# Time mixing of an eight-stage network on one core: one product per batch on GpSimd, two denominators on GpSimd, residual on TensorE or VectorE

## The reference, cut to what matters

```
xn = ln(x);  xx = shift(xn)                       # previous position
k = mix(xn, xx, mu_k) @ Wk;  v = ... @ Wv;  r = sigmoid(... @ Wr)
scan over positions, per batch and channel, carry (aa, bb, pp):
    qq  = max(pp, u + k);   e1 = exp(pp - qq);   e2 = exp(u + k - qq)
    wkv = (e1*aa + e2*v) / (e1*bb + e2)
    qq2 = max(pp + w, k);   e1b = exp(pp + w - qq2);   e2b = exp(k - qq2)
    aa, bb, pp = e1b*aa + e2b*v,  e1b*bb + e2b,  qq2
x = x + (r * wkv) @ Wo
ei = ln(x)                                        # feeds the expert layer
```

## Time and profile before

| | |
|---|---|
| median of 3 runs | 1217.03 us (1211.10 to 1218.83) |
| the profiled execution | 1211.25 us, of which 1208.9 us from the first to the last instruction |
| mean granted TensorE clock | 0.981 |
| PE busy | 1102.3 us (91%) |
| DVE busy | 931.1 us (77%) |
| ACT busy | 812.0 us (67%) |
| POOL busy | 234.9 us (19%) |

### The profile page before, as it was taken

One profiled execution on the slowest core, in us unless ns is written; L12 is line 12 of the kernel. 1 busy time (PEld: TensorE's weight loads), 2 busy tenths in 40 slices (PEclk: granted clock), 3 DMA queues, 4 the chain that ended last, 5 costly groups with the idle time before them and its releaser, 6 DMA issues.

```text
span 1208.9 us, 20220 instructions
## 1 busy us (share of the span) xinstructions
PE 1102.3 (91%) x7428; PEld 614.3 (51%) x7436; DVE 931.1 (77%) x1521; ACT 812.0 (67%) x1292; POOL 234.9 (19%) x332
## 2 busy tenths in 40 slices
PE   7978899999999989989999899898888888898987
PEld 3333344444444445467765354466666666463354
DVE  5997798777777677767775578699999896576966
ACT  6885655555555654755576646888888776868774
POOL 1000000000000001200000013487878776000000
PEclk9999999999999999989999999899999998999999
DMA  6000112121221000000000000000000000000002
GB/s 177 1 0 1 56 56 67 65 62 61 62 61 61 27 1 0 10 1 2 2 1 1 1 0 9 1 3 2 2 3 2 16 2 2 9 1 1 1 1 69
DMA packets 26361, 27.17 MB, mean 22 GB/s; under 512 B 4171, under 2 KB 17308, under 8 KB 26268
## 3 DMA queue, kind: packets, MB, share of 16 engines
q1 hardware_dynamic: 25936, 25.91, 7.3%
q10 hardware_dynamic: 332, 0.01, 0.0%
HBM read 23.30 MB, written 2.62 MB: 21 GB/s over the span
## 4 chain that ended last, share of the span: by engine, by line
PE 61%; DVE 19%; ACT 12%; issue 6%; POOL 1%; DMA 0%; ACTq 0%; DVEq 0%
PE psum L723 9%; PE psum L734 9%; PE psum L726 4%; PE psum L87 4%; PE psum L983 4%; PE psum L955 3%; PE psum L1634 2%; PE psum L1965 2%; DVE arena L2151 2%; PE psum L1382 2%; DVE N L2160 2%; ACT ln_std L114 2%; ACT ln_std L116 2%; PE psum L105 1%; ACT N L2065 1%
## 5 line engine op out<-in xcount | busy, mean ns | idle before, releaser
L762 ACT ACTIVATE arena<-psum 128x512 f32<-128x512 f32 x128 | 69.5, 594 | 114.5 <-PE psum L723 114.5
L723 PE MATMUL psum<-arena,weights 128*128 128x512 f32 x256 | 122.2, 600 | 1.7 <-DVE N L128 1.0
L734 PE MATMUL psum<-arena,weights 128*128 128x512 f32 x256 | 120.3, 592 | 0.0
L620 DVE SCALAR_TENSOR_TENSOR arena<-diff,vecs,N 128x512 f32<-128x512 f32 x128 | 95.1, 745 | 0.0
L682 DVE SCALAR_TENSOR_TENSOR arena<-arena,psum 128x512 f32<-128x512 f32 x64 | 43.9, 686 | 62.8 <-PE psum L734 62.8
L2065 ACT ACTIVATE N<-N 128x1024 f32<-128x1024 f32 x64 | 67.8, 1059 | 32.2 <-DVE N L2160 31.6
L1975 PE MATMUL psum<-ident,N 128*128 128x128 f32 x512 | 73.0, 288 | 13.3 <-POOL N L2120 12.7
L723 PEld LDWEIGHTS psum<-arena,weights 128*128 128x128 f32 x256 | 48.2, 191 | 62.4 <-issue 57.9
L734 PEld LDWEIGHTS psum<-arena,weights 128*128 128x128 f32 x256 | 48.6, 190 | 61.4 <-issue 61.4
L1965 PE MATMUL psum<-arena 32*128 32x128 f32 x1024 | 77.2, 290 | 1.6 <-ACT arena L2043 1.4
L2061 ACT ACTIVATE arena<-psum 128x1024 f32<-128x1024 f32 x64 | 65.6, 1024 | 19.2 <-PE psum L1975 19.0
(11 more groups left out here) (330 smaller groups left out, 2491.0 us busy)
## 6 DMA issues: line engine op xcount, KB each, us to landing
arena<-tw_rows SPq DMA_DIRECT2D x64, 256.0 KB, 3.1
out_dram<-arena SPq DMA_DIRECT2D x8, 256.0 KB, 3.6
arena<-in_L_attn_a_x_dram SPq DMA_DIRECT2D x3, 512.0 KB, 6.7
weights<-in_L_attn_a_eWk_dram SPq DMA_DIRECT2D x1, 1024.0 KB, 6.0
arena<-in_L_attn_a_x_dram SPq DMA_DIRECT2D x2, 256.0 KB, 3.9
weights<-in_L_attn_a_eWr_dram SPq DMA_DIRECT2D x1, 512.0 KB, 9.9
tw_rows<-arena SPq DMA_DIRECT2D x2, 128.0 KB, 2.7
tw_rows<-arena SPq DMA_DIRECT2D x1, 256.0 KB, 3.5
```

The source lines that it names most:

```text
L620: op = nc.vector.scalar_tensor_tensor(mixed[:, n % 4, a, :], k.diff[:, q % 2, :], k.vec((f"cm_k{e}", f"cm_r{e}")[a]), before, ALU.mult, AL ...
L723: op = nc.tensor.matmul(k.bank[2 * (n % 2) + h][:], k.eWk[:, e, h * P:(h + 1) * P], mixed[:, n % 4, 0, :], start=True, stop=True)
L734: op = nc.tensor.matmul(k.bank[4 + n % 2][:], k.eWv[:, e, h, :], ks[:, (2 * (n % 2) + h) * CH:(2 * (n % 2) + h + 1) * CH], start=(h == 0), ...
L762: op = nc.scalar.activation(kr[:, h * CH:(h + 1) * CH], k.bank[2 * (n % 2) + h][:], ACT.Relu)
```

## The change

- VectorE no longer makes e2*V (L443). GpSimd makes it, for all four batches, once d(b) is done (so p is free), V(b) is taken and the last exponential of batch b is there. VectorE's numerator (L445) waits for it through a new semaphore, `wkv_part`.
- For batches 2 and 3 GpSimd also adds e2 to e1*bb in place, and `over` reads that sum from SBUF. den(2) and den(3) are gone from TensorE, and `totals[b]` is used for b = 0 and 1 only.
- On TensorE, den(0) still follows K3, then come V3, R0, den(1), R1, R2, R3. On ScalarE, the takes of V3 and R0 to R3 stand between the last weights, each one or more places earlier.
- The residual: for batches 0 and 1 TensorE first multiplies Y by the identity into `backs[b]` and adds Wo's product onto it, and ScalarE copies the sum to Y (`keep`); for batches 2 and 3 VectorE adds as before, counted by a new semaphore, `wkv_added`. On VectorE the four results now stand one behind another.
- The second norm's waits are renumbered accordingly.

```diff
--- before.py
+++ after.py
@@ -307,9 +307,7 @@
                 nc.tensor.matmul(k.bank[n % 4][:], k.wA[:, j, :], before, start=False, stop=True).then_inc(k.kvr, 1)
 
         def den(b):
-            total = totals[b % 2]
-            if b >= 2:
-                pe.wait_ge(k.wkv_ln, b - 1)
+            total = totals[b]
             pe.wait_ge(k.wkv_exp, 4 * b + 4)
             for c in range(2):
                 nc.tensor.matmul(total[:, c * CH:(c + 1) * CH], k.ident[:], e2[b % 2][:, c * CH:(c + 1) * CH], start=True, stop=False)
@@ -319,23 +317,25 @@
             op.then_inc(k.wkv_total, 1)
 
         def out(b):
-            pe.wait_ge(*((k.kvr_out, 2 * len(place)) if b < 2 else (k.wkv_ln, b + 1)))
+            pe.wait_ge(*((k.kvr_out, 2 * len(place)) if b < 2 else (k.wkv_ln, b - 1)))
+            if b < 2:
+                for c in range(2):
+                    nc.tensor.matmul(backs[b][:, c * CH:(c + 1) * CH], k.ident[:], k.Y[:, half[b][c]], start=True, stop=False)
             pe.wait_ge(k.wkv_out, b + 1)
             for c in range(2):
-                nc.tensor.matmul(backs[b][:, c * CH:(c + 1) * CH], k.wA[:, 3, :], R[:, half[b][c]], start=True, stop=True).then_inc(k.wkv_prod, 1)
+                nc.tensor.matmul(backs[b][:, c * CH:(c + 1) * CH], k.wA[:, 3, :], R[:, half[b][c]], start=(b >= 2), stop=True).then_inc(k.wkv_prod, 1)
 
         pe.wait_ge(k.mix_fold, 6)
         pe.wait_ge(k.pads_set, 2 * B)
         for kind, b in (("K", 0), ("K", 1), ("V", 0), ("V", 1), ("K", 2), ("V", 2), ("K", 3)):
             mix(kind, b)
         den(0)
+        mix("V", 3)
+        mix("R", 0)
         den(1)
-        mix("V", 3)
-        for b in range(B):
+        for b in range(1, B):
             mix("R", b)
-        den(2)
         out(0)
-        den(3)
         out(1)
         for c in range(2):
             after.center(pe, c)
@@ -372,10 +372,15 @@
             nc.scalar.activation(buf, buf, ACT.Exp, scale=-1.0).then_inc(k.wkv_exp, 1)
 
         def over(b):
-            act.wait_ge(k.wkv_total, b + 1)
-            nc.scalar.activation(K[:, at[b]], totals[b % 2], ACT.Ln, scale=2.0).then_inc(k.wkv_ln, 1)
+            act.wait_ge(*((k.wkv_total, b + 1) if b < 2 else (k.wkv_part, 2 * b)))
+            nc.scalar.activation(K[:, at[b]], totals[b] if b < 2 else e1b[b % 2], ACT.Ln, scale=2.0).then_inc(k.wkv_ln, 1)
             act.wait_ge(k.wkv_ln, b + 1)
             nc.scalar.activation(K[:, at[b]], K[:, at[b]], ACT.Exp, scale=-1.0).then_inc(k.wkv_rden, 1)
+
+        def keep(b):
+            for c in range(2):
+                act.wait_ge(k.wkv_prod, 2 * b + c + 1)
+                nc.scalar.activation(k.Y[:, half[b][c]], backs[b][:, c * CH:(c + 1) * CH], ACT.Copy).then_inc(k.wkv_y, 1)
 
         take("K", 0)
         take("K", 1)
@@ -391,28 +396,40 @@
             weight(1, n)
         take("V", 2)
         take("K", 3)
-        for n in range(4):
-            weight(2, n)
+        weight(2, 0)
+        weight(2, 1)
+        take("V", 3)
+        weight(2, 2)
+        weight(2, 3)
+        take("R", 0)
         weight(3, 0)
         weight(3, 1)
-        take("V", 3)
-        take("R", 0)
+        take("R", 1)
         weight(3, 2)
-        take("R", 1)
+        take("R", 2)
         weight(3, 3)
-        take("R", 2)
         take("R", 3)
         activations(act, k, "natural_log_exp_and_others")
-        over(0)
-        over(1)
-        over(2)
+        for b in range(B):
+            over(b)
+        keep(0)
         act.wait_ge(k.wkv_num, B - 1)
-        act.wait_ge(k.wkv_total, B - 1)
         for c in range(2):
             after.square(act, c)
-        over(3)
+        keep(1)
         for c in range(2, 4):
             after.square(act, c)
+
+    @block.gpsimd
+    def _(pool):
+        for b in range(B):
+            pool.wait_ge(k.wkv_d, b + 1)
+            pool.wait_ge(k.kvr_out, 2 * place[f"V{b}"] + 2)
+            pool.wait_ge(k.wkv_exp, 4 * b + 4)
+            nc.gpsimd.tensor_tensor(p[b % 2], e2[b % 2], V[:, at[b]], ALU.mult).then_inc(k.wkv_part, 1)
+            if b >= 2:
+                pool.wait_ge(k.wkv_e1bb, b + 1)
+                nc.gpsimd.tensor_tensor(e1b[b % 2], e1b[b % 2], e2[b % 2], ALU.add).then_inc(k.wkv_part, 1)
 
     @block.vector
     def _(dve):
@@ -433,15 +450,14 @@
             nc.vector.tensor_tensor_scan(bb[:, 1:L + 1], e1b[s], e2b[s], 0.0, ALU.mult, ALU.add).then_inc(k.wkv_step, 1)
             dve.wait_ge(k.kvr_out, 2 * place[f"V{b}"] + 2)
             nc.vector.tensor_tensor(aa[:, 1:L + 1], e2b[s], V[:, at[b]], ALU.mult).then_inc(k.wkv_step, 1)
-            dve.wait_ge(k.wkv_step, 5 * b + 2)
+            dve.wait_ge(k.wkv_step, 4 * b + 2)
             nc.vector.tensor_tensor_scan(aa[:, 1:L + 1], e1b[s], aa[:, 1:L + 1], 0.0, ALU.mult, ALU.add).then_inc(k.wkv_step, 1)
-            dve.wait_ge(k.wkv_step, 5 * b + 3)
+            dve.wait_ge(k.wkv_step, 4 * b + 3)
             dve.wait_ge(k.wkv_exp, 4 * b + 3)
             nc.vector.tensor_tensor(e1b[s], e1[s], bb[:, 0:L], ALU.mult).then_inc(k.wkv_e1bb, 1)
             nc.vector.tensor_tensor(e2b[s], e1[s], aa[:, 0:L], ALU.mult).then_inc(k.wkv_step, 1)
-            dve.wait_ge(k.wkv_exp, 4 * b + 4)
-            nc.vector.tensor_tensor(p[s], e2[s], V[:, at[b]], ALU.mult).then_inc(k.wkv_step, 1)
-            dve.wait_ge(k.wkv_step, 5 * b + 5)
+            dve.wait_ge(k.wkv_part, max(b + 1, 2 * b - 1))
+            dve.wait_ge(k.wkv_step, 4 * b + 4)
             nc.vector.tensor_tensor(V[:, at[b]], e2b[s], p[s], ALU.add).then_inc(k.wkv_num, 1)
 
         def result(b):
@@ -465,7 +481,7 @@
         def add(b):
             for c in range(2):
                 dve.wait_ge(k.wkv_prod, 2 * b + c + 1)
-                nc.vector.tensor_tensor(k.Y[:, half[b][c]], k.Y[:, half[b][c]], backs[b][:, c * CH:(c + 1) * CH], ALU.add).then_inc(k.wkv_y, 1)
+                nc.vector.tensor_tensor(k.Y[:, half[b][c]], k.Y[:, half[b][c]], backs[b][:, c * CH:(c + 1) * CH], ALU.add).then_inc(k.wkv_added, 1)
 
         arguments(0)
         arguments(1)
@@ -475,12 +491,8 @@
         arguments(3)
         sums(2)
         sums(3)
-        result(0)
-        result(1)
-        add(0)
-        result(2)
-        add(1)
-        result(3)
+        for b in range(B):
+            result(b)
         add(2)
         add(3)
 
@@ -623,7 +635,7 @@
 
     def before_up(pe, c):
         if c == 5:
-            pe.wait_ge(k.wkv_y, 2 * B)
+            pe.wait_ge(k.wkv_added, B)
             logits(pe, 0)
         if c == 7:
             turn_logits(pe, 0)
...
@@ mixed_out and mixed_free in all_norms @@
     def mixed_out(pe, c):
-        pe.wait_ge(k.wkv_y, c + 1)
+        pe.wait_ge(*((k.wkv_y, c + 1) if c < W else (k.wkv_added, c + 1 - W)))
 
     def mixed_free(pe, c):
         if c < 3:
-            pe.wait_ge(k.wkv_y, c + 5)
+            pe.wait_ge(k.wkv_added, c + 1)
...
```

More of the change, by code:

```diff
@@ L2288 @@
 MOE_SEMS = ["mix_fold", "kvr", "kvr_out", "wkv_w", "wkv_init", "wkv_pp", "wkv_d", "wkv_relu", "wkv_exp", "wkv_step", "wkv_e1bb", "wkv_num",
-            "wkv_total", "wkv_gated", "wkv_ln", "wkv_rden", "wkv_out", "wkv_prod", "wkv_y", "rt_prod", "rt_copied", "rt_turned", "rt_weights", "rt_wT", "rt_back",
+            "wkv_total", "wkv_gated", "wkv_ln", "wkv_rden", "wkv_out", "wkv_prod", "wkv_y", "wkv_added", "wkv_part", "rt_prod", "rt_copied", "rt_turned", "rt_weights", "rt_wT", "rt_back",
             "rt_step", "rt_exps", "rt_const", "ex_stored", "ex_diff", "ex_mix", "ex_r", "ex_v", "ex_tanh", "ex_added", "ex_gate",
@@ L2533, in build @@
                 (k.mix_fold, k.kvr, k.kvr_out, k.wkv_w, k.wkv_init, k.wkv_pp, k.wkv_d, k.wkv_relu, k.wkv_exp, k.wkv_step, k.wkv_e1bb, k.wkv_num,
-                 k.wkv_total, k.wkv_gated, k.wkv_ln, k.wkv_rden, k.wkv_out, k.wkv_prod, k.wkv_y, k.rt_prod, k.rt_copied, k.rt_turned, k.rt_weights,
+                 k.wkv_total, k.wkv_gated, k.wkv_ln, k.wkv_rden, k.wkv_out, k.wkv_prod, k.wkv_y, k.wkv_added, k.wkv_part, k.rt_prod, k.rt_copied, k.rt_turned, k.rt_weights,
                  k.rt_wT, k.rt_back, k.rt_step, k.rt_exps, k.rt_const, k.ex_stored, k.ex_diff, k.ex_mix, k.ex_r, k.ex_v,
```

## The result

| | before | changed |
|---|---|---|
| median of 8 runs | 1217.38 us | 1223.90 us |
| the profiled execution | 1211.25 us | 1223.35 us |
| first scan of VectorE to first gate | 57.12 us | 64.99 us |
| first scan to the first variance matmul | 74.63 us | 81.22 us |

The account below looks back on a forecast made before the run. The prediction took a sum of VectorE instructions as the bound up to 94.39 us, then a tail. Its terms, -4.56 + 12.30 - 2.84 + 1.72 = +6.6 us on the median 1217.03, gave 1223.6 us, range 1210 to 1229.

Parts of the forecast that it names:

- Part 2: VectorE's chain before the gates: six 128x1024 GpSimd instructions, 2.05 us each, add their whole length to it, +12.30 us.
- Rival 1: VectorE's scans: GpSimd gets through beside them, 3.7 us less, so +2.9 us and 1219.9 us; chance 0.18.
- Rival 3: GpSimd's 1024-column instructions: each much longer than two short ones, about 2.96 us or more, 1229.1 us and above; chance 0.09.
- rival 2: VectorE beside GpSimd: no conflict, the product is simply taken off, -5.7 us, 1211.3 us; chance 0.11.
- Part 1: VectorE's chain: the product e2*V leaves it, 1.14 us in each of four batches, -4.56 us.
- Part 3: New order on ScalarE and TensorE: cost 0, inverses ready before VectorE asks, the 2.59 us wait of result(3) gone.
- Part 4: Tail from gate to first variance matmul: bound by TensorE's seven 1.72 us blocks, 14.67 us against 17.51, -2.84 us.
- Part 5: TensorE before out(0): its clock falls in some 13.5 us of idling, +1.72 us on the tail, bounds 0 and 1.9.
- The sum: Whole kernel: all terms together +6.6 us, added to the median of before, 1217.03 us, giving 1223.6 us.
- the first three cases: GpSimd beside VectorE: full stop (chance 0.62, 1223.6 us), scans let through (0.18, 1219.9 us), no conflict (0.11, 1211.3 us).

Follow-up runs that it names:

- own first: Changed kernel with batch 1's identity product moved ahead of out(0): scan to variance 79.63 us, median 1223.79 us, ratio 1.0042 to the kernel before.
- kept busy: Changed kernel with TensorE repeating batch 0's identity product seven more times before out(0): scan to variance 79.83 us, median 1225.57 us, ratio 1.0085 to before.
- left out: Changed kernel with GpSimd's six instructions shortened to 128x1: scan to gate 52.86 us, scan to variance 70.38 us, median 1222.30 us.
- sums only: Changed kernel with e2*V back on VectorE, GpSimd making only the two sums: scan to variance 78.04 us, median 1229.44 us, ratio 1.0085 to before.
- products only: Changed kernel with den(2) and den(3) back on TensorE, GpSimd making only the four products: scan to gate 61.04 us, median 1222.54 us.

## Why the prediction was right, and where it was lucky

- **Part 2, the full stop.** Forecast 12.30 us, measured 12.13, or 2.02 for each of six; 1.89 and 2.09 were its bounds; the 2.25 that the prediction set beside its own figure as an estimate was too long. Rival 1 fell with one row, the scan of 4.43 us, and with GpSimd's rows of 3.62 and 3.87 us, which waited for scans. Here the Trainium skill's page "SBUF — State Buffer" (section "Who interferes with whom") was right in both halves: the second one in blocks fully (the trace agrees, by the ends of the rows above), and a GpSimd instruction that only writes does not contend (VectorE keeps 1.20 and 2.29 us beside a memset). Rival 3 is out, d being 2.02, and rival 2 is out with the rows and with the kernel that only leaves the work out.
- **Part 1.** 4.26 of 4.56. Most of the missing 0.30 stands ahead of the numerator: it begins 1.32 us behind the instruction before it (L458 to L461), where it had begun 1.26 behind (L443 to L445), four times. It has one more semaphore to wait for, GpSimd's; that this is the reason no run shows.
- **Part 3.** ScalarE's first two inverses were ready at 94.6, the fourth at 103.5; forecast 94.5 and 104.3. It never held VectorE.
- **Part 4.** 14.67 us forecast from gate to variance, 16.23 - 1.69 (clock) = 14.54 measured; own first removes the block that I named.
- **Part 5.** 1.72 forecast, 3.41 - 1.72 = 1.69 measured. That the size fits is partly luck: in seven of the eight variants (all but kept busy) such a restart cost 1.8 to 3.3 us, after idle times of 3.6 to 12.2 us. The bounds, 0 and 1.9, were too narrow above.
- **The sum.** +6.6 forecast, +6.59 in the stage, where small errors of the terms cancel. That the medians differ by +6.5 as well is luck: with the same remainder of the network, the kernel with GpSimd's work left out has a stage 10.84 us shorter than the changed one and a median only 1.60 lower. Taking the median of before and not the profiled execution as the base was right for a reason that I did not know: that execution had fewer falls of the clock in a stage far behind. And the range of 1210 to 1229 was so wide that a time inside it would not have told the first three cases apart; the stage does.
- **A sign that did show.** The prediction called itself wrong if the stage behind 112 us shifted by something else than the variance matmul does. Up to the attention stage it shifts by the same 6.6 us, behind it by 12.5 in the two traces. The part of the prediction that everything behind moves with that matmul therefore did not hold in the profiled executions; executions of one kernel differ by as much among themselves (before: 1211.10 to 1229.64 us).
- **Wrong in detail.** I expected GpSimd's rows near 2.05 us; they are 2.53 to 3.87, as a row holds its waiting too. And the sum of batch 2 got in behind L458, not L457.

## What to carry to other kernels

Before a VectorE instruction is handed to GpSimd, look at what both read. If VectorE is the bound and its instructions read two SBUF tensors, and GpSimd's reads SBUF too, GpSimd's length is added to VectorE's. GpSimd takes 2.0 us for what VectorE does in 1.14, so the move of a product loses about 1.0 each time (four products: 61.04 - 57.12 = 3.92). What the traces here show running side by side undisturbed are GpSimd instructions that only write, VectorE instructions with one of two operands in PSUM, and those with a single input, in SBUF, as the reduction of 901.23 in the kernel before. It begins beside the GpSimd product of 900.74, which runs to 901.80, and takes the same 0.68 us as at 778.58, where GpSimd is idle:

```profile
778.58 0.68 DVE L2167 TENSOR_REDUCE arena<-N 128x32 f32<-128x512 f32 x1
...
901.23 0.68 DVE L2167 TENSOR_REDUCE arena<-N 128x32 f32<-128x512 f32 x1
```

Reorder the queues first: here the stage was 3.35 us shorter by order alone. And when a gain of 0.3% is looked for in a kernel whose clock falls here and there, measure the stage in the trace; ten runs of the whole did not see it.

## What the runs showed of the hardware that was not expected

- The stop goes by instruction, however small. In the kernel that leaves GpSimd's work out, its six instructions of a single column took from 0.22 to 1.10 us. Each was issued while a two-input VectorE instruction was under way, and each ended within 0.06 us of that instruction's end: the first of the two here at 80.16, where VectorE's ended at 80.11, the second at 84.81, where VectorE's ended at 84.76. So even the 0.22 us may hold waiting. GpSimd first, then VectorE:

```profile
79.06 1.10 POOL L432 TENSOR_TENSOR ln_sq<-ln_sq,ln_std 128x1 f32<-128x1 f32 x1 [4.80 <-DVE ln_sq L457]
84.59 0.22 POOL L429 TENSOR_TENSOR arena<-arena 128x1 f32<-128x1 f32 x1 [4.43 <-ACT arena L372]
```

```profile
78.89 1.22 DVE L458 TENSOR_TENSOR ln_sq<-ln_std,mixed 128x1024 f32<-128x1024 f32 x1
...
83.56 1.20 DVE L452 TENSOR_TENSOR mixed<-arena 128x1024 f32<-128x1024 f32 x1
```

- TensorE's restart after idling is not one price. After 12.18 us (sums only) the first block took 3.78 us and the next 1.93; after 4.34 us (left out) 3.78 and 2.83; after 3.02 us before the change 1.98. In the changed kernel the clock fell once more where nothing waited for it: TensorE had idled 3.55 us before 82.54, its first matmuls still ran at 0.91 or more, and from 84 to 87, with TensorE busy throughout, the granted clock was 0.50. What picks between these cases no run here shows.
- The remainder of the network, identical in all kernels, took from 1045.5 us (products only) to 1068.3 (left out) from the variance matmul to the last table load in the profiled executions, at mean clocks of 0.980 and 0.955. Whether the shift of a stage by some us makes such falls likelier is open: the changed kernel's eight runs lie at 0.962 to 0.966, 31 runs of the kernel before, beside the first four variants, at 0.965 to 0.979, and the variants show both. The lowest of the eight runs lie 12.0 us apart (1211.10 and 1223.13), twice what the stage explains.
